# Unit 24 of the adjacency matrix goes through the transposing DMA too, and the loads and sums around it are put in another order

## The reference

```python
x, adj        # x is 2048 x 512, adj is 2048 x 2048, both float32
h = relu(layernorm(x))
x = x + (adj @ quantised(relu(quantised(h) @ quantised(weight))))   # with scale factors
h = relu(layernorm(x))
S = (adj + adj.T) * 0.5 + eye(2048)          # D = diagonal of the row sums of S
x = x + (adj @ (D**-0.5 @ S @ D**-0.5)) @ h
```

## Time and profile before

| | |
|---|---|
| median of three runs | 494.21 us |
| the profiled execution, its own time | 493.84 us |
| its span | 492.0 us |
| TensorE busy | 478.2 us, 97% of the span |
| VectorE busy | 268.4 us |
| ScalarE busy | 154.5 us |
| GpSimd busy | 47.3 us |
| TensorE clock granted | 0.999 |

### The profile page before, as it was taken

One profiled execution on the slowest core, in us unless ns is written; L12 is line 12 of the kernel. 1 busy time (PEld: TensorE's weight loads), 2 busy tenths in 40 slices (PEclk: granted clock), 3 DMA queues, 4 the chain that ended last, 5 costly groups with the idle time before them and its releaser, 6 DMA issues.

```text
span 492.0 us, 6358 instructions
## 1 busy us (share of the span) xinstructions
PE 478.2 (97%) x2358; PEld 232.0 (47%) x2358; DVE 268.4 (55%) x360; ACT 154.5 (31%) x300; POOL 47.3 (10%) x54
## 2 busy tenths in 40 slices
PE   2899999999999999999999999999999999999997
PEld 2655444444544444444444444444444444444446
DVE  5967997779998788876997777240100001000010
ACT  1887834867651354353521211230000000000000
POOL 2321953223100000000000000000000000000000
PEclk9999999999999999999999999999999999999999
DMA  8986999999794332323232321054000000100001
GB/s 303 403 319 161 224 218 248 215 233 255 178 302 191 89 126 87 125 87 99 85 117 93 121 85 43 0 183 180 36 29 21 21 21 21 43 21 21 21 23 43
DMA packets 62507, 62.65 MB, mean 127 GB/s; under 512 B 45464, under 2 KB 45720, under 8 KB 62488
## 3 DMA queue, kind: packets, MB, share of 16 engines
q1 hardware_dynamic: 62480, 62.40, 43.5%
q10 hardware_dynamic: 8, 0.00, 0.0%
HBM read 42.99 MB, written 8.39 MB: 104 GB/s over the span
## 4 chain that ended last, share of the span: by engine, by line
PE 92%; DVE 3%; DMA 2%; ACT 1%; SPq 1%; issue 1%; POOL 0%; ACTq 0%
PE ps_a L1202 32%; PE ps_p L1100 20%; PE ps_p L1165 8%; PE ps_a L1165 7%; PE ps_b L1165 7%; PE ps_h L1165 4%; PE ps_m L1165 4%; DMA feat<-in_x 2%; PE ps_b L1051 1%; PE ps_h L1100 1%; PE ps_m L1100 1%; DVE small L942 1%; PE ps_b L1218 1%; PE ps_a L1218 1%; PE ps_a L1051 1%; PE ps_a L1079 1%
## 5 line engine op out<-in xcount | busy, mean ns | idle before, releaser
L1100 PE MATMUL ps_p<-small,at 128*128 128x512 f16 x448 | 99.1, 379 | 0.0
L1020 DVE SCALAR_TENSOR_TENSOR feat<-ps_a,feat 128x512 f32<-128x512 f32 (+1 forms) x16 | 10.8, 675 | 148.7 <-PE ps_a L1202 144.2
L1202 PE MATMUL ps_a<-small,at 128*128 128x512 f16 x360 | 80.1, 379 | 0.0
L1202 PE MATMUL ps_a<-a_in,at 128*128 128x512 f16 x360 | 80.1, 379 | 0.0
L1100 PEld LDWEIGHTS ps_p<-small,at 128*128 128x128 f16 x448 | 43.7, 98 | 50.2
L585 ACT ACTIVATE split<-a_in 128x1024 f16<-128x1024 f32 x30 | 31.7, 1057 | 101.8 <-PE ps_p L1165 90.0
L938 DVE TENSOR_TENSOR split<-a_in,split 128x1024 f16<-128x1024 f32 x30 | 36.7, 1224 | 34.1 <-ACT split L585 34.1
L1202 PEld LDWEIGHTS ps_a<-small,at 128*128 (+1 forms) x360 | 35.2, 98 | 42.5
L1202 PEld LDWEIGHTS ps_a<-a_in,at 128*128 (+1 forms) x360 | 35.2, 98 | 42.5
L1165 PE MATMUL ps_p<-feat,split 128*128 (+1 forms) x180 | 43.9, 379 | 0.5 <-DVE small L942 0.5
L1165 PE MATMUL ps_a<-feat,split 128*128 (+1 forms) x180 | 43.8, 379 | 0.0
(11 more groups left out here) (182 smaller groups left out, 436.2 us busy)
## 6 DMA issues: line engine op xcount, KB each, us to landing
a_in<-in_adj SPq DMA_DIRECT2D x46, 512.0 KB, 3.9
at<-in_adj SPq DMA_DIRECT2D x16, 512.0 KB, 8.6
out<-feat SPq DMA_DIRECT2D x31, 256.0 KB, 4.2
feat<-in_x SPq DMA_DIRECT2D x8, 512.0 KB, 11.1
feat<-out SPq DMA_DIRECT2D x4, 1024.0 KB, 9.4
at<-in_L_gnn_weight SPq DMA_DIRECT2D x2, 512.0 KB, 3.9
split<-in_adj SPq DMA_DIRECT2D x1, 512.0 KB, 16.3
tmp<-in_adj SPq DMA_DIRECT2D x1, 512.0 KB, 16.4
```

The lines of the kernel that those rows point to most:

```text
L1020: nc.vector.scalar_tensor_tensor(out, products, 1.0 / (SA * SZ), out, ALU.mult, ALU.add).then_inc(y_out, 1)
L1100: last = nc.tensor.matmul(l0_bank(r), at_block(r, lo, j), small[:, j * D:(j + 1) * D], start=(j == 0 and lo == 0), stop=(j == T - 1 and lo ...
L1202: last = nc.tensor.matmul(BANK[n], at_block(t, lo, j), z_part(j, z_lo), start=(j == 0 and lo + z_lo == 0), stop=(j == T - 1 and lo == 1))
```

## The change

Unit 24 is moved and no longer turned: stage 10 has no `turn`, and stage 9 moves three units. Units 14 to 19 are loaded in a row between the moves of 3 and 5; before, 14 and 15 came after the move of 5 and 16 to 19 one by one behind later moves. Unit 17 is made ready in stage 5 and no longer in stage 6. The columns of units 10 and 14 are summed by VectorE in stages 5 and 7 and no longer by ScalarE, and the other column sums stand earlier. `sum_unit(1)` stands in stage 9 and no longer in stage 10, `sum_lo(1)` in 10 and no longer in 11, and `sum_hi(0)`, `sum_hi(1)` stand ahead of `hi_rows` in stages 9 and 10.

```diff
-EVEN = (10, 12, 14, 18, 20, 22, 26)
+EVEN = (10, 12, 14, 18, 20, 22, 24, 26)
+SUMMED_LATE = (10, 14)
...
-        MOVES = {1: [9], 2: [10, 11], 3: [12], 4: [13, 14], 5: [15], 6: [17, 18], 7: [19, 20], 8: [21, 22],
-                 9: [23, 25], 10: [26], 11: [27, 29]}
+        MOVES = {1: [9], 2: [10, 11], 3: [12], 4: [13, 14], 5: [15, 17], 6: [18], 7: [19, 20], 8: [21, 22],
+                 9: [23, 24, 25], 10: [26], 11: [27, 29]}
...
-        SUMS_OF = {5: [[(10, FIRST)], [], [(10, LAST)]], 7: [[(12, FIRST)], [(12, LAST)], []],
...
+        SUMS_OF = {7: [[(12, FIRST)], [(12, LAST)], []], 8: [[(18, FIRST)], [(18, LAST)], []],
...
             move(3)
+            sp.wait_ge(sq_ready, T // 2)
+            for u in range(14, AHEAD):
+                rows(u)
             move(5)
-            sp.wait_ge(sq_ready, T // 2)
-            rows(14)
-            rows(15)
             move(7)
...
+                if r in (9, 10):
+                    sum_hi(r - 9)
...
-                if r == 9:
-                    sum_hi(0)
-                if r == 11:
-                    sum_hi(1)
...
+                for k, u in enumerate(SUMMED_LATE):
+                    if r == (5, 7)[k]:
+                        wait_moved(dve, u)
+                        column_sum_late(u)
...
                 if r == 9:
                     sum_lo(0)
+                    sum_unit(1)
                 if r == 10:
-                    sum_unit(1)
-                if r == 11:
                     sum_lo(1)
```

More of the change, by code:

```diff
@@ L287, in gnn_kernel @@
         ROW_SUMS = {2: [0], 4: [1, 2, 4], "acc": []}
-        MOVES = {1: [9], 2: [10, 11], 3: [12], 4: [13, 14], 5: [15], 6: [17, 18], 7: [19, 20], 8: [21, 22],
-                 9: [23, 25], 10: [26], 11: [27, 29]}
+        MOVES = {1: [9], 2: [10, 11], 3: [12], 4: [13, 14], 5: [15, 17], 6: [18], 7: [19, 20], 8: [21, 22],
+                 9: [23, 24, 25], 10: [26], 11: [27, 29]}
         ADD_AT = {u: (u - 7) // 2 for u in ADDED if u >= 9}
         FIRST, LAST = range(0, B // 2), range(B // 2, B)
-        SUMS_OF = {5: [[(10, FIRST)], [], [(10, LAST)]], 7: [[(12, FIRST)], [(12, LAST)], []],
-                   8: [[(14, FIRST)], [(14, LAST)], []], 9: [[(18, FIRST)], [(18, LAST)], []],
-                   10: [[], [], [(20, FIRST)]], 11: [[], [(20, LAST)], [(22, FIRST)]],
-                   12: [[], [], [(22, LAST), (26, FIRST)]], 13: [[], [], [(26, LAST)]]}
+        SUMS_OF = {7: [[(12, FIRST)], [(12, LAST)], []], 8: [[(18, FIRST)], [(18, LAST)], []],
+                   9: [[(20, FIRST)], [(20, LAST)], []], 10: [[(22, FIRST)], [], [(22, LAST)]],
+                   11: [[], [], [(24, FIRST), (24, LAST)]], 12: [[], [], [(26, FIRST), (26, LAST)]]}
         PARTS = sum(len(place) for places in SUMS_OF.values() for place in places)
@@ L368, in _ @@
             move(3)
+            sp.wait_ge(sq_ready, T // 2)
+            for u in range(14, AHEAD):
+                rows(u)
             move(5)
-            sp.wait_ge(sq_ready, T // 2)
-            rows(14)
-            rows(15)
             move(7)
-            LOADS = {9: [16], 10: [17], 11: [18], 12: [19], 13: [20], 14: [21], 15: [22], 17: [23], 20: [24], 21: [25], 22: [26],
-                     23: [27], 25: [29, 28], 26: [30], 27: [31]}
+            LOADS = {13: [20], 14: [21], 15: [22], 17: [23], 20: [24], 21: [25], 22: [26], 23: [27], 24: [28], 25: [29],
+                     26: [30], 27: [31]}
             for r in range(1, 12):
@@ L379, in _ @@
                     for w in LOADS.get(u, []):
[L380 to L383, removed]
+                        rows_again(w)
             for v in range(2, 6):
@@ L969, in _ @@
             link(nc.vector.memset(pause[:, :], 0.0))
+            late_sums = colp[:, :].rearrange("p (u b) -> p u b", b=B)[:, SUMMED_LATE[0]:SUMMED_LATE[-1] + 1:4, :]
+            nc.vector.tensor_scalar(late_sums, late_sums, 1.0 / SA, None, ALU.mult)
             link(nc.vector.tensor_scalar(colp[:, a:b], colp[:, a:b], 1.0 / SA, None, ALU.mult))
@@ L976, in _ @@
             for moved_sums in (rs3[:, ADDED[1] // 2:ADDED[-1] // 2 + 1, 1],
-                               rs3[:, 5:14:2, 0], rs3[:, 6:11:4, 0]):
+                               rs3[:, 5:14:2, 0], rs3[:, 6, 0:1], rs3[:, 10:13:2, 0]):
                 last = nc.vector.tensor_scalar(moved_sums, moved_sums, 1.0 / SA, None, ALU.mult)
```

## The result

In eleven runs of each, in turn on the same chip, the kernel before took a median of 494.04 us (492.97 to 495.52) and the changed kernel 496.08 us (494.88 to 497.44). The ratio is 1.0041, with an interval of 1.0027 to 1.0056: slower by 2.0 us, where 0.9 us less was forecast. The profiled execution took 497.44 us with a span of 495.6 us, one of the two longest of the eleven, so its sum has to be made against its own time, 3.60 us above that of the profiled execution before, and then against the median.

What follows compares the result with a forecast made beforehand. TensorE was taken as the bound in stages 1 to 13. -0.87 - 0.22 + 0.2 = -0.89 us, from a median of 494.21, forecast 493.3 us; range 492.8 to 495.0.

Steps and rivals of the forecast that it cites:

- `turn(24)` is -0.87: TensorE, stage 10: dropping this turn was claimed as a certain gain of 0.87 us.
- the wait before `turn(30)`: TensorE waiting for lo_turned(28) to free the bank: claimed to vanish with sum_unit(1) earlier, -0.22 us.
- `sum_unit(1)` ahead of `x1_tile(9)`: VectorE before layer0(11): x1_tile(9) claimed 0.8 us in time, so the step costs nothing.
- the cover is that 0.3: VectorE: third piece of sum_unit(1) counted to start 0.3 us ahead of GpSimd's addition of 27.
- rival B: Stages 8 and 9 late on ScalarE, sum_blocks(18) awaiting the move of 18: layer0(11) +2.1, total 495.2 us; chance 0.12.
- A: GpSimd's addition of 27 gets the port before sum_unit(1)'s last piece: layer0(11) +1.3, total 494.4 us; chance 0.27.
- Column sums: nothing: VectorE's late sums in stages 5 and 7 claimed to fit where it waits for TensorE, at no cost.
- The load of 14 to 19 ahead of the move of 5: nothing.: Before layer0(2)'s ninth matmul: unit 5 claimed to land at 55.8, needed at 56.5, so no cost.
- rival C: Unit 5 late for layer0(2), as six loads share memory worse: +0.3 to +0.8 us, 493.6 to 494.1; chance 0.08.
- The wait for `acc`, +0.2: TensorE before turn("acc"): a new wait for the addition of 29, taken as +0.2 us, between 0 and +1.2.
- the landing of the load of 29: SP queue: load counted as issued at 120.66 and landed at 124.96, making acc ready at 127.3.
- the loads of 24 to 27: SP queue from stage 9: claimed to be issued about 1.03 us earlier each, that of 27 at 111.94.

Runs made afterwards that it cites:

- e8: The kernel before with only the second product's sums moved earlier (sum_unit(1), sum_lo(1), sum_hi(0), sum_hi(1)): 493.47 us, ratio 0.9982.
- e1: The changed kernel with sum_unit(1) directly behind x1_tile(9) in stage 10 instead of ahead of it: 495.30 us, ratio 1.0023.
- e2: The changed kernel with only units 14 and 15 loaded ahead of the move of 5, 16 to 19 behind that of 7: 495.54 us, ratio 1.0037.
- e3: The changed kernel with GpSimd's addition of unit 27 made to wait for x1_tile(9): 496.46 us, ratio 1.0048.
- e12: The changed kernel with unit 24 turned again as before and its other edits kept: 495.15 us, ratio 1.0021.
- e14: The changed kernel with unit 24 turned again and only two loads ahead of the move of 5: 493.73 us, ratio 0.9995.
- e7: The kernel before with only the loads of 14 to 19 put together between the moves of 3 and 5: 494.69 us, ratio 1.0017.
- e5: The changed kernel with sum_unit(1), sum_lo(1), sum_hi(0) and sum_hi(1) back where they stood before: 498.38 us, ratio 1.0086.
- e6: The changed kernel with the second product's sums back, two loads ahead of the move of 5, load of 29 straight behind that of 28: 497.23 us, ratio 1.0052.

## Why the prediction was wrong

*The steps that held.* `turn(24)` is -0.87 and the wait before `turn(30)` -0.22, in the changed kernel and, for the second, in e8.

*The step that failed: "`sum_unit(1)` ahead of `x1_tile(9)` [...] I cost this step at nothing; the cover is that 0.3".* It measured +2.43. The count began at `sum_unit(0)` ending at 104.53, the time of before, and nothing had made sure of that: I had rival B beside it, in which `sum_blocks(18)` waits for the move of 18, and gave it 0.12. That move landed at 96.8, past the 95.3 from which B begins to count. So B made VectorE 1.6 us late, and A, the port, added 2.0: the third piece came 1.6 us later than counted, the addition of 27 only 1.1 later (117.36, not 116.3), and the cover of 0.3 was gone. They are one chain, where I had them as rivals with a chance each. B was right in its mechanism and in its size: from 96.1 it counted `layer0(11)` at 119.9, and 0.7 more gives the measured 120.6. e1, e2 and e3 each took away one link, and the wait was gone or 0.3 us.

*The step under it that failed too: "Column sums: nothing".* It put VectorE's late sums where "it now waits for TensorE for a microsecond or two". In stage 5 that idle time was 1.18 us, and `lo_rows(17)` (1.1 us) and the late sum of unit 10 (2.2 us) were put into it. VectorE, before and after:

```profile
82.43 0.75 DVE L882 SCALAR_TENSOR_TENSOR feat<-ps_p,cst,feat 128x512 f32<-128x512 f32 x1 [1.18 <-PE ps_p L1100]
```

```profile
80.64 4.46 DVE L747 TENSOR_REDUCE colp<-at 128x8 f32<-128x2048 f16 x2
85.03 0.73 DVE L877 SCALAR_TENSOR_TENSOR feat<-ps_p,cst,feat 128x512 f32<-128x512 f32 x1
```

`x1_tile(5)` is 2.6 us late by it (0.5 of that is TensorE's own), `lo_rows(18)` behind it ends at 90.07, and the chain after runs through all of these into the move of 18. The move took 6.7 us from issue to landing, near the 6.9 of the earlier trace rows; the load of 23 ahead of it was issued at 88.38 and left the queue free at 88.91, so a move that had not waited for `lo_rows(18)` could have gone out 1.2 us earlier (an estimate from these rows). The other half is the four blocks of `sum_blocks(18)` on ScalarE, 1.6 us. e12 and e14 have the same column sums, and ScalarE waits for the move of 18 in both (4.5 and 4.6 us); their TensorE does not wait for it; they have `turn(24)` on TensorE and one `lo_rows` less in stage 9. This is read from the records: no run changes the column sums alone.

*"The load of 14 to 19 ahead of the move of 5: nothing."* It measured +0.49, rival C, within its bound of +0.3 to +0.8. The six landed 1.5 us apart, not 1.3, the last at 54.90. Over many executions the step is worse than in this one: 1.3 us between e12 and e14.

*The wait for `acc`, +0.2,* did not show in the changed kernel, as its TensorE was late already. It shows as 0.5 to 3.0 us when the earlier wait is mended. Mis-sized was the landing of the load of 29, at 127.3 against 124.96: it was issued at 121.78, 1.1 us later than counted, and took 5.5 us instead of 4.3. The 1.1 us had arisen early: I counted the loads of 24 to 27 as going out 1.03 us earlier than before, and that of 27 went out at 112.97, exactly as before.

*A term that was missing.* I priced a wait by its length. In two executions of eleven the 2.4 us of idle TensorE were followed by 3.4 us at the lower clock, +1.70 more. The profiled execution has this term and lies 1.4 us above the median.

*The sum:* -0.87 - 0.22 + 0.49 + 2.43 = +1.83 beside a median of +2.04. The range went by these terms and ended at 495.0, a microsecond short. It was said to leave out "the far part of B", but B's own figure was 495.2: all of B lay outside it.

## What to carry to other kernels

Work saved on the bound engine is worth its time only if nothing that it is traded for stands within the jitter of a transfer from being due: here 0.87 us of TensorE were exchanged for one more DMA between two loads, whose landings vary by 2 us, and margins of 0.3 to 1.3 us were used up in three places. When a count starts from a time of the kernel before, first ask what the change does to that time, and make one case of rivals that lie in one chain. Try the parts apart: the one that looked like a mere consequence (e8) was the only one with a gain clear of its interval. And idle time on an engine off the critical path is no free room: here 1.2 us of it were given 3.3 us of work, and 30 us later TensorE waited.

## What the hardware showed

- Three loads of 512 KB into `a_in` took 4.3, 5.5 and 6.2 us (units 27, 29 and 23) in one and the same execution. A transposing move issued straight behind six loads landed 9.7 us later (9.6 in e7, 11.9 in e12), against 6.9 behind two.
- In the profiled execution the granted clock was 0.50 for about 3.4 us after some 2.3 us of idle TensorE; in e3's it was 0.50 behind a wait of 2.9 us, and in e2's the mean stayed at 1.000 with a wait as long. Of the changed kernel two executions of eleven show a mean of 0.997 or less; where in them the clock fell is seen only in the profiled one. e5 had such a mean in 3 of 4 and e6 in 6 of 10, both with waits of over 2 us before `turn(30)`; e12, with 2.3 us in `layer0(2)`, and the kernels without a wait (e8, e14) in none.
- The kernels without a wait spread least: e8 covers 1.5 us and e14 1.1 us in ten and eleven runs, e3 6.1 us in eight. The rule is loose, as the kernel before, with a wait of 0.2 us, covers 2.6 us in its eleven. Part of it arises early: `layer0(2)` started at 54.62 in the changed kernel and at 55.76 in e1, whose program is the same up to there; that is 1.1 of the 1.5 us by which e1's profiled execution is longer than that of the kernel before.
